# Mixer output projection: four fp32 matmuls of the unrounded y instead of twelve fp32r matmuls of its rounded halves, in a chunk's first slot

## The reference, cut to what matters

```python
y = ssd_scan(xh, dt, Bm, Cm, A)
y = y + D_skip[None, None, :, None] * xh
y = y.reshape(*y.shape[:-2], D_INNER)          # 512 wide
y = y * jax.nn.silu(z)
y = y * jax.lax.rsqrt(jnp.mean(jnp.square(y), axis=-1, keepdims=True) + 1e-05) * rms_w
return y @ out_proj_w                          # 512 -> 256
```

## Time and profile before

| what | value |
|---|---|
| median of three runs | 3421.74 us (3414.98 to 3423.02) |
| the profiled execution's own time | 3418.95 us |
| its span, first to last instruction | 3417.2 us |
| mean granted TensorE clock | 0.927 of full |
| TensorE matmul busy | 2913.7 us (85%) |
| VectorE busy | 2058.8 us (60%) |
| ScalarE busy | 1260.0 us (37%) |
| GpSimd busy | 909.8 us (27%) |
| mixer with preparation | until about 1434 us |

### The profile page before, as it was taken

The page is one execution under the profiler, slowest core; times in us unless marked ns, Lnnn a source line. Parts: engine busy times, 40 slices in busy tenths (PEclk is TensorE's granted clock), DMA queues, the critical chain, the costliest instruction groups (busy, mean ns, idle before and its releaser), DMA issues. The chain is left out here.

```text
span 3417.2 us, 46659 instructions
## 1 busy us (share of the span) xinstructions
PE 2913.7 (85%) x17254; PEld 2225.1 (65%) x17254; DVE 2058.8 (60%) x3922; ACT 1260.0 (37%) x1978; POOL 909.8 (27%) x796
## 2 busy tenths in 40 slices
PE   0688888888888888776776769999999999999999
PEld 0455555555555555566665658787878787878787
DVE  4899999999989998655556543333333333333333
ACT  0555555555555555343344332222222222222222
POOL 5032323332333233322222222222222222222222
PEclk6799999999889999888888889999999999999999
DMA  3000101010101010133111110000000000000000
GB/s 126 19 27 25 33 19 33 19 32 19 33 19 32 19 32 27 62 129 114 39 59 39 39 45 1 17 11 19 11 18 12 16 14 14 10 17 12 16 14 13
DMA packets 104860, 107.11 MB, mean 31 GB/s; under 512 B 35896, under 2 KB 98616, under 8 KB 102976
## 3 DMA queue, kind: packets, MB, share of 16 engines
q1 hardware_dynamic: 99520, 103.81, 9.3%
q10 hardware_dynamic: 5120, 0.19, 0.1%
HBM read 71.41 MB, written 40.94 MB: 33 GB/s over the span
## 5 line engine op out<-in xcount | busy, mean ns | idle before, releaser
L1582 PE MATMUL fbank<-hid,fw 128*128 128x512 f32 x4096 | 962.3, 395 | 0.0
L1582 PEld LDWEIGHTS fbank<-hid,fw 128*128 128x128 f32 x4096 | 766.1, 187 | 187.0
L1732 DVE TENSOR_TENSOR hid<-fhf,hid 128x512 fp32r<-128x512 f32 x384 | 265.0, 690 | 704.2 <-POOL hid L1689 704.2
L1689 POOL TENSOR_SCALAR hid<-fhf 128x512 fp32r<-128x512 f32 x384 | 271.0, 706 | 1044.1 <-ACT fhf L1661 760.8
L803 ACT ACTIVATE mh<-ebank 128x512 f32<-128x512 f32 x512 | 303.3, 600 | 586.6 <-PE ebank L658 585.5
L672 PE MATMUL yin<-mh,xpad 128*32 128x128 f32 x4096 | 346.7, 292 | 101.9 <-DVE mh L1094 100.8
L1094 DVE SCALAR_TENSOR_TENSOR mh<-mh,gm 128x512 f32<-128x512 f32 x512 | 397.7, 783 | 3.1 <-ACT mh L803 3.0
L672 PEld LDWEIGHTS yin<-mh,xpad 128*32 128x32 f32 x4096 | 198.3, 113 | 267.8 <-DVE mh L1094 144.9
L645 PE MATMUL ebank<-ah,win 128*128 128x512 f32 x640 | 246.2, 424 | 6.7 <-DVE al L988 3.6
L1042 DVE SCALAR_TENSOR_TENSOR xc<-cin,cw,xc 128x512 f32<-128x512 f32 x288 | 240.6, 836 | 0.2
L1661 ACT ACTIVATE fhf<-fbank,sh2c 128x512 f32<-128x512 f32 x128 | 88.0, 688 | 382.4 <-PE fbank L1582 382.4
(11 more groups left out here) (184 smaller groups left out, 4859.8 us busy)
## 6 DMA issues: line engine op xcount, KB each, us to landing
fx<-x_d SPq DMA_DIRECT2D x17, 512.0 KB, 3.9
xs<-in_x SPq DMA_DIRECT2D x16, 512.0 KB, 4.3
h_d<-in_h SPq DMA_DIRECT2D x16, 512.0 KB, 5.2
o_d<-o SPq DMA_DIRECT2D x16, 512.0 KB, 3.1
mo<-o_d SPq DMA_DIRECT2D x16, 512.0 KB, 3.8
mx<-in_x SPq DMA_DIRECT2D x16, 512.0 KB, 4.7
x_d<-mx SPq DMA_DIRECT2D x16, 512.0 KB, 2.8
fw<-h_d SPq DMA_DIRECT2D x2, 4096.0 KB, 15.0
```

The costliest lines, as they stand in the source:

```text
L1582: mm = pe.matmul(bank[banks.slot(key)][:], w[:, k, m * P:(m + 1) * P].bitcast(dt), h[:, k, :].bitcast(dt), start=(k + n == 0), stop=(k == ...
L1689: pool.tensor_scalar(hid[i % 2][0][:, m, :], hf[j % 3][:], 1.0, 0.0, ALU.mult, ALU.add)\
L1732: dve.tensor_tensor(hid[i % 2][1][:, m, :], hf[j % 3][:], hid[i % 2][0][:, m, :].bitcast(F32), ALU.subtract).then_inc(c_lo.sem, 1)
```

## The change

- `project(q)` runs four fp32 matmuls of the gated y itself and of one unrounded `wout`, each 128x128 by 256 columns, in place of the twelve fp32r ones. It waits for the gated y (`c_yg`). The four matmuls on the squares stay.
- `yh` and `yl` with their instructions (ScalarE L865, GpSimd L918) and semaphores go; VectorE's preparation of `wout` is the scaling alone.
- On TensorE `project(q - 2)` stands at i = 0 instead of i = 7: for a chunk seven slots earlier, and in the sequence of a chunk's steps behind `intra` and ahead of `state_decay`, and ahead of the block's first input transposes where n = 0. The bank order has `op` first at i = 0 accordingly; the cyclic order of the five products stays.
- ScalarE's `y_out`, now the square alone, stands at i = 0 instead of 1. VectorE's `square_mean` and `residual` are for chunk q - 1 at i = 6 and 7 instead of q - 2 at 5 and 6; GpSimd's `rms_power` for q - 1 at i = 6.
- GpSimd's `gated(q)` waits for the projection of chunk q - 1 instead of for its square and `yl`.
- SyncE's wait and store of `o1` stand ahead of `decay_left(i + 1)` and `decay_right(4i + 3)`.
- `LAST` is seven slots less.

```diff
--- before.py
+++ after.py
@@ -131,7 +131,7 @@
 LAG = 5
 MH = 7
 FIRST = -SPAN
-LAST = (CHUNKS + 2) * NG
+LAST = (CHUNKS + 1) * NG + 1
 
 NT_AT = (0, 1)
 AFFINE_AT = (1, 2)
@@ -195,6 +195,8 @@
     for S in range(FIRST, LAST):
         q, i = divmod(S, NG)
         n, j = S % SPAN, S // SPAN + 1
+        if i == 0 and has_chunk(q - 2):
+            yield ("op", q - 2)
         if i == 1 and has_off(q - 1):
             yield ("yoff", q - 1)
         if i == 2 and has_state(q - 1):
@@ -203,8 +205,6 @@
             yield ("xT", q + 1)
         if i == 6 and has_chunk(q + 1):
             yield ("bt", q + 1)
-        if i == 7 and has_chunk(q - 2):
-            yield ("op", q - 2)
         if j < BLOCKS and n == DTW_AT:
             yield ("dtw", j)
 
@@ -286,7 +286,7 @@
 
 
     win = [sb(f"win{j}", [P, KD, ZX], F32R) for j in range(2)]
-    wout = [sb(f"wout{j}", [P, QI, D], F32R) for j in range(2)]
+    wout = sb("wout", [P, QI, D])
     wdt = sb("wdt", [P, KD, NH])
     cw = sb("cw", [P, XM, TAPS])
     cb = sb("cb", [P, XM])
@@ -314,8 +314,6 @@
     c_yread = Count(sem, "yin_read", 0)
     c_yused = Count(sem, "addends_used", 0)
     c_yg = Count(sem, "y_gated", 0)
-    c_yh = Count(sem, "y_hi_made", 0)
-    c_yl = Count(sem, "y_lo_made", 0)
     c_ysq = Count(sem, "y_squared", 0)
     c_mean = Count(sem, "square_mean_made", 0)
     c_rms = Count(sem, "rms_made", 0)
@@ -362,7 +360,7 @@
         s_store = sem("s_store")
         s_a = sem("s_a")
         splits = [(g["w_in"][:, 0:ZX].rearrange("(k p) n -> p k n", p=P), win, KD, ZX),
-                  (g["w_out"].rearrange("(k p) n -> p k n", p=P), wout, QI, D),
+                  (g["w_out"].rearrange("(k p) n -> p k n", p=P), None, QI, D),
                   (g["m1"].rearrange("(k p) n -> p k n", p=P), wm1, KD, FF),
                   (g["m2"].rearrange("(k p) n -> p k n", p=P), wm2, KF, D)]
         block = own.enter_context(nc.Block())
@@ -450,9 +448,9 @@
                 if i == 1:
                     dve.wait_ge(s_vec, 16)
                     for q in range(k):
-                        last = dve.tensor_scalar(w[:, q, :], w[:, q, :], rmsw[:, q:q + 1], None, ALU.mult)
-                    last.then_inc(s_const, 1)
-                    dve.wait_ge(s_const, 2)
+                        last = dve.tensor_scalar(wout[:, q, :], w[:, q, :], rmsw[:, q:q + 1], None, ALU.mult)
+                    last.then_inc(s_split, 2)
+                    continue
                 dve.tensor_copy(halves[0][:], w).then_inc(s_split, 1)
                 dve.wait_ge(s_split, 2 * i + 1)
                 dve.tensor_tensor(halves[1][:], w, halves[0][:].bitcast(F32), ALU.subtract).then_inc(s_split, 1)
@@ -532,8 +530,6 @@
     yin_s = sb("yin_s", [P, QI, P])
     yg = sb("yg", [P, QI, P])
     ysq = sb("ysq", [P, QI, P])
-    yh = sb("yh", [P, QI, P], F32R)
-    yl = sb("yl", [P, QI, P], F32R)
     ms = sb("ms", [P, 1])
     rms = sb("rms", [P, 1])
     o1 = sb("o1", [P, NC, D])
@@ -612,13 +608,13 @@
             for i in blocks:
                 decay_right(NC * i + 1)
                 decay_right(NC * i + 2)
-                if i + 1 < BLOCKS:
-                    decay_left(i + 1)
-                decay_right(NC * i + 3)
                 if i:
                     released(sp, ("op", NC * i - 1))
                     sp.dma_start(o1_d[(i - 1) // NU, rows_of(i - 1), :].rearrange("(c p) d -> p c d", p=P), o1[:])\
                         .then_inc(c_stored.sem, 16)
+                if i + 1 < BLOCKS:
+                    decay_left(i + 1)
+                decay_right(NC * i + 3)
                 if i + 1 < BLOCKS:
                     decay_right(NC * i + 4)
                 if i + 3 < BLOCKS:
@@ -685,11 +681,10 @@
 
             def project(q):
                 key = ("op", q)
-                pe.wait_ge(c_yl.sem, c_yl.at(0, q + 1))
+                pe.wait_ge(c_yg.sem, c_yg.at(0, q + 1))
                 o = fresh(key)
                 for f in range(QI):
-                    product(o[:, 0:D], [y[:, f, :] for y in (yh, yl)], [w[:, f, :] for w in wout],
-                            f == 0, f == QI - 1)
+                    pe.matmul(o[:, 0:D], yg[:, f, :], wout[:, f, :], start=(f == 0), stop=(f == QI - 1))
                 pe.wait_ge(c_ysq.sem, c_ysq.at(0, q + 1))
                 for f in range(QI):
                     mm = pe.matmul(o[:, D:D + 1], ysq[:, f, :], ones[:, 0:1], start=(f == 0), stop=(f == QI - 1))
@@ -771,6 +766,8 @@
                     decay(q, i)
                 if has_chunk((S - LAG) // NG):
                     intra(*divmod(S - LAG, NG))
+                if i == 0 and has_chunk(q - 2):
+                    project(q - 2)
                 if i == 1 and has_off(q - 1):
                     state_decay(q - 1)
                     from_state(q - 1)
@@ -780,8 +777,6 @@
                     x_by_token(q + 1)
                 if i == 6 and has_chunk(q + 1):
                     b_by_token(q + 1)
-                if i == 7 and has_chunk(q - 2):
-                    project(q - 2)
                 if j < BLOCKS:
                     if n in NT_AT:
                         transposes(j, NT_AT.index(n))
@@ -862,7 +857,6 @@
                 act.wait_ge(c_yg.sem, c_yg.at(0, q + 1))
                 if q:
                     made(act, ("op", q - 1))
-                nc.scalar.activation(yh[:], yg[:], ACT.Copy).then_inc(c_yh.sem, 1)
                 nc.scalar.activation(ysq[:], yg[:], ACT.Square).then_inc(c_ysq.sem, 1)
 
             for S in range(FIRST, LAST):
@@ -870,7 +864,7 @@
                 n, j = S % SPAN, S // SPAN + 1
                 if has_chunk(q):
                     exponent(q, i)
-                if i == 1 and has_chunk(q - 2):
+                if i == 0 and has_chunk(q - 2):
                     y_out(q - 2)
                 if i == 2 and has_off(q - 1):
                     state_decay(q - 1)
@@ -901,8 +895,7 @@
             def gated(q):
                 added(pool, q)
                 if q:
-                    pool.wait_ge(c_ysq.sem, c_ysq.at(0, q))
-                    pool.wait_ge(c_yl.sem, c_yl.at(0, q))
+                    made(pool, ("op", q - 1))
                 if has_off(q):
                     pool.tensor_tensor(yg[:], yin_s[:], yoff_s[:], ALU.add).then_inc(c_yused.sem, 1)
                 else:
@@ -913,23 +906,17 @@
                     pool.wait_ge(c_xc.sem, c_xc.at(0, q // NC + 1))
                 pool.tensor_tensor(yg[:], yg[:], sz[q // NC % 2][:, :, tokens(q)], ALU.mult).then_inc(c_yg.sem, 1)
 
-            def y_low(q):
-                pool.wait_ge(c_yh.sem, c_yh.at(0, q + 1))
-                pool.tensor_tensor(yl[:], yg[:], yh[:].bitcast(F32), ALU.subtract).then_inc(c_yl.sem, 1)
-
             power(1)
             power(2)
             for S in range(FIRST, LAST):
                 q, i = divmod(S, NG)
                 n, j = S % SPAN, S // SPAN + 1
-                if i == 0 and has_chunk(q - 2):
-                    y_low(q - 2)
                 if j + 1 < BLOCKS and n in LN_POW_AT:
                     power(2 * (j + 1) + LN_POW_AT.index(n) + 1)
                 if i == 2 and has_chunk(q - 1):
                     gated(q - 1)
-                if i == 5 and has_chunk(q - 2):
-                    rms_power(q - 2)
+                if i == 6 and has_chunk(q - 1):
+                    rms_power(q - 1)
 
         @block.vector
         def _(dve):
@@ -1157,10 +1144,10 @@
                     x_by_token(q + 1)
                 if i == 4 and has_chunk(q + 1):
                     b_by_token(q + 1)
-                if i == 5 and has_chunk(q - 2):
-                    square_mean(q - 2)
-                if i == 6 and has_chunk(q - 2):
-                    residual(q - 2)
+                if i == 6 and has_chunk(q - 1):
+                    square_mean(q - 1)
+                if i == 7 and has_chunk(q - 1):
+                    residual(q - 1)
                 if j < BLOCKS:
                     if n in AL_AT:
                         low(j, AL_AT.index(n))

```

## The result

Seven runs of the changed kernel gave 3431.99 us (3427.31 to 3435.47) beside 3416.10 us (3411.39 to 3427.68) of the kernel before: ratio 1.0037, 95% interval 1.0024 to 1.0051. Later, beside other runs of the kernel before, it was 0.9991 (0.9979 to 1.0002). In that later series two executions, one of each kernel, at a granted clock of 0.55 and 0.64, took 4764 and 4166 us and are left out.

A forecast was written before the change was run, and what follows sets the result against it. VectorE was taken as the bound through most of a block, TensorE at two places. Per block -1.56 + 0.4 - 1.5 = -2.66 us, 16 blocks -42.6, with preparation -44.5: median 3377 us, range 3336 to 3409.

The forecast's parts named there:

- Part 1: TensorE's projection: four fp32 matmuls take 1.92 us, 0.43 us more than twelve fp32r ones, covered where VectorE is the bound.
- Part 2: VectorE's lock beside yl: 1.56 us a block gained at slots 6 and 22, nothing at 31, +0.4 at 14.
- Part 3: ScalarE's work before affine at the block's end: of TensorE's 1.22 us wait, 0.8 us gained.
- Part 4: Block's end: moved projection fills TensorE's idle time, half clock goes or shortens; with ScalarE's gain -1.5 us a block.
- rival A: TensorE keeps full clock, VectorE's waits for it go, three locks gained: -5.8 us a block, 3327 us; chance 0.15.
- Part 5: Moved readers, bank order and store cost 0; TensorE reaches the projection two slots before VectorE asks.
- Part 6: One-time effects: preparation of wout gains 1.9 us; the very end is even, within 3 us.
- B: Slot 0 projection waits 1 us or more for gated y, half clock stays: -0.6 us a block, 3411 us; chance 0.17.
- C: TensorE becomes the bound in slots 8 to 20 and the block's end: slower, 3448 us; chance 0.09.

The follow-up runs named there:

- experiment 6: Four fp32 matmuls in slot 7 with each projection run twice into the same bank: ratio 1.0132 to the kernel before, against 0.9864 with each run once.
- experiment 5: Four fp32 matmuls in slot 7 plus an unread GpSimd subtraction per chunk where yl was made: ratio 0.9970 to the kernel before, against 0.9864 without it.
- Experiment 4: Changed kernel with the projection ahead of the intra products, still in slot 0: 3396.51 us, ratio 0.9917 to the kernel before.
- experiment 3: Changed kernel with mean square, power and output rows one slot later: 3444.25 us, ratio 1.0071 to the kernel before.
- Experiment 7: Changed kernel with only the last five chunks projected in slot 7 and read as before, gated y double-buffered: 3397.81 us, ratio 0.9941 to the kernel before.
- Experiment 1: Change's four fp32 matmuls, but projection and readers in the slots of before, gated y double-buffered: ratio 0.9865 to the kernel before, again 0.9864.

## Why the prediction was wrong

**Part 1, the fp32 projection: right.** Forecast 1.92 us. At full clock eight records take 1.84 us start to start, so 0.35 us more than the fp32r form, not 0.43. Two rows of the changed kernel, to set beside the earlier trace rows:

```profile
1396.14 1.99 PE L687 MATMUL bank<-wout,yg 128*128 128x256 f32 x8 [1.83 <-POOL yg L907]
1397.98 0.95 PE L690 MATMUL bank<-ones,ysq 128*128 128x1 f32 x8
```

Its cover was overrated: I let it count in one place of a block and the block's end; experiment 6 has 77% on the path.

**Part 2, the lock: right in kind, too small.** VectorE lost 3.6 us of busy time a block (forecast 10 to 15 us in four, measured 14.6); experiment 5 shows it worth 36 us by itself, forecast 25 (1.56 x 16). The exclusive lock of the Trainium skill (SBUF — State Buffer, "Who interferes with whom") fits. Its bound of the full 1.28 us each would be 82 us; the chip says 44% of that.

**Part 3, ScalarE: the wait right, the gain not.** The wait of the second transposes fell from 1.22 to 0.18 us. But they start 9.0 us after the mask of slot 27 instead of 7.0 (547.76 less 538.72, 547.53 less 540.51), so nothing was gained there.

**Part 4, the block's end: this step failed.** Forecast for it and part 3 -1.5 us a block; at the end read above the state update came 2.0 us later after the mask than before. I asked whether the gated y would be there, but not what stands in front of the projection in its new slot: the intra products with their mask wait. Slot 31's projection filled that wait, slot 0's comes behind it. Experiment 4 gives this order alone 2.7 us a block (82.62 less 79.92) and 41 us in all.

The half clock did not go either. The projection that was to fill the idle stretch ran ahead of it, from 519.25 to 521.89, and the clock fell at 533.9 after this:

```profile
523.10:533.90 10.80, 6.89 (x59) 3.73 (x59) 10.57 (x27) 9.47 (x9) 2.58 (x2) 1.00 0.00 0
```

That is 6.9 us of 10.8, where it had been 6.7; and slot 0's projection lay in the half clock as slot 31's had. I had also taken it that less idle time means more clock. In the four blocks TensorE's idle time fell from 47.0 us to 37.7, and the clock from 0.93 to 0.91. In experiment 4 it is 39.4 us idle at 0.96:

```profile
462.00:790.00 328.00, 288.63 (x2118) 189.46 (x2117) 302.56 (x655) 171.03 (x282) 77.85 (x57) 0.96 0.09 27
```

The Trainium skill has the clock follow TensorE's recent activity (TensorE: Matmul & The Clock Gate, "The HAM clock gate"), and rival A leaned on it. The fall at 533.9 agrees with it; the means of four blocks do not order the clocks, so it could not be used on them.

**Part 5, the readers: a false reading too, but by itself it cost little that shows.** I wrote that TensorE reaches the projection "when VectorE is in slots 3 to 4, two slots before it asks". That holds where TensorE has its full lead of five slots. At a block's end it has not: VectorE asks in slot 30 and TensorE is still in slot 32's projection; 2.21 us. I had the lead by slot from the waits and did not look it up at the one place where VectorE already waited for TensorE. In the steady blocks this wait is the sign of part 4's error and not a second cause: moving the readers only moved it (experiment 3), and with the order repaired it went with the readers where they were (experiment 4).

**Part 6.** The preparation gave 1.5 us (first mask at 136.7, now 135.2; forecast 1.9). From the last mask to the last output rows it takes 13.5 us, before 13.9: even, as forecast. But between the two the last block lost 12 us, for which the sum had no term, since I counted sixteen equal blocks. The last one, without input projections and with less to cover TensorE, is another regime: the gated y is not there when TensorE comes (13.7 us in all), and VectorE then waits for the squares. Experiment 7 takes this away by moving projection and readers back together, so it does not part the two; later readers alone (62.3 us) or the other order alone (61.9 us) did not help. In the changed kernel's second trace the loss is 5.7 us and not 12 (55.4 against 49.7).

**The rivals.** B was the nearest: it has TensorE wait for the gated y in slot 0, and that is what the last block shows (13.7 us). In the steady blocks only its half clock on the projection came true, not the wait for y, and its price of 3411 us is near the second measurement by luck. C (TensorE as the bound everywhere) was wrong: its waits for masks are still 4.9 us a block.

## What to carry to other kernels

When work is moved among fixed slots, look up the order inside the new slot and the lead of each engine at that slot, chunk by chunk and in the last block apart; a mean lead says nothing at the one place where the follower already waits. A wait in the list is not yet a cause: one edit that removes it alone (experiment 3) shows whether it only moves. Work that fills another instruction's wait is free only in front of it. And an engine that is mostly idle can still cost time through the port that it shares with VectorE: here 1.28 us of GpSimd cost VectorE's path 0.56.

## What the runs showed of the hardware that was not expected

**Who gets the port is not a property of the kernel.** Experiment 1, the same kernel twice, VectorE and GpSimd in slot 17 to 18, first trace:

```profile
580.77 1.78 DVE L1082 SCALAR_TENSOR_TENSOR mh<-mh,gm 128x512 f32<-128x512 f32 x1
582.47 1.76 DVE L1030 SCALAR_TENSOR_TENSOR xc<-cin,cw,xc 128x512 f32<-128x512 f32 x1
```

```profile
580.32 1.68 POOL L901 TENSOR_TENSOR yg<-yin_s,yoff_s 128x512 f32<-128x512 f32 x1 [9.04 <-DVE yin_s L1092]
```

And the second:

```profile
579.42 0.69 DVE L1082 SCALAR_TENSOR_TENSOR mh<-mh,gm 128x512 f32<-128x512 f32 x1
580.03 1.79 DVE L1030 SCALAR_TENSOR_TENSOR xc<-cin,cw,xc 128x512 f32<-128x512 f32 x1
```

```profile
578.99 2.28 POOL L901 TENSOR_TENSOR yg<-yin_s,yoff_s 128x512 f32<-128x512 f32 x1 [9.04 <-DVE yin_s L1092]
```

In the first the mask took 1.78 us beside GpSimd's add; in the second it took its 0.69 and the add stretched to 2.28. It is not which of them started first: the add starts 0.44 to 0.45 us ahead of the mask in both, and so it does at this place in the 14 blocks of each of the thirteen traces. Of the 14 blocks, the mask was the long one in 10 to 14 up to experiment 4 and in none or one after it, so single blocks go either way, and the chip or the hour sets how often. What settles it was not tried.

It need not cost what it seems to. In experiment 1 slot 18 became 1.0 us shorter, but the block only 0.19 (80.09 to 79.90), since slot 0 took 0.66 us more. In the changed kernel the block went from 82.62 to 81.74.

The dearest case is the last chunk but one of the changed kernel. VectorE's five masks, GpSimd's add and TensorE's projection, first trace:

```profile
1422.77 3.09 DVE L1081 SCALAR_TENSOR_TENSOR mh<-mh,gm 128x512 f32<-128x512 f32 x5
...
1422.98 3.99 POOL L900 TENSOR_TENSOR yg<-yin_s,yoff_s 128x512 f32<-128x512 f32 x1 [6.54 <-DVE yin_s L1091]
...
1428.37 3.57 PE L687 MATMUL bank<-wout,yg 128*128 128x256 f32 x8 [3.62 <-POOL yg L907]
```

And the second:

```profile
1404.82 5.23 DVE L1081 SCALAR_TENSOR_TENSOR mh<-mh,gm 128x512 f32<-128x512 f32 x5
...
1405.04 1.59 POOL L900 TENSOR_TENSOR yg<-yin_s,yoff_s 128x512 f32<-128x512 f32 x1 [6.54 <-DVE yin_s L1091]
...
1408.36 1.99 PE L687 MATMUL bank<-wout,yg 128*128 128x256 f32 x8 [0.49 <-POOL yg L907]
```

In the first the five masks ran at full speed and the add ended only behind the last of them, after 3.99 us. The gated y came late, TensorE idled 3.62 us and then had half its clock for nearly all of the projection, and VectorE waited 6.90 us for the squares instead of 1.12. In the second the add took 1.59 us and two masks 1.75 us each, and all the rest came sooner. From the first of the five masks to the next one behind the wait it is 10.1 us in the first trace (1422.77 to 1432.84) and 6.4 in the second (1404.82 to 1411.25): 3.6 of the 6.1 us by which the last 31 masks differ. Here VectorE's winning the port was the loss.

So the changed kernel is "0.4% slower" in one series and "the same" in another, 1.0037 and 0.9991, a distance beyond the interval of either: an interval from one series does not cover it.
